# Attention without context in a stage of its own, with all scores of an item at once

## The reference

```
q, k, v = x Wq, x Wk, x Wv              (16 heads of 16; two of the blocks have biases)
s = q k^T / sqrt(16)                    (per head, 128 x 128)
s = s - slope(head) * |row - column|    (second block), or the causal mask (first and third)
p = softmax(s);  a = p v;  y = a Wo + bo + residual
```

## Time and profile before

| what | value |
|---|---|
| median of 3 runs (lowest, highest) | 3216.21 us (3214.78, 3226.16) |
| the profiled execution | 3218.95 us, span 3217.0 us |
| TensorE products busy | 2769.1 us, 86% of the span |
| VectorE, ScalarE, GpSimd busy | 1649.4, 1451.8, 1388.2 us |
| first stage, 1205 to 1400 us: TensorE, VectorE, ScalarE, GpSimd busy; granted clock | 175.55, 101.67, 132.59, 103.69 us; 0.98 |
| second stage, 1735 to 1925 us: the same | 166.08, 135.47, 146.49, 112.75 us; 0.92 |
| third stage, 2720 to 2912 us: the same | 179.34, 106.34, 138.51, 113.24 us; 0.98 |

### The profile page before, as it was taken

The page is one execution under the profiler, slowest core; times in us unless marked ns, Lnnn a source line. Parts: engine busy times, 40 slices in busy tenths (PEclk is TensorE's granted clock), DMA queues, the critical chain, the costliest instruction groups (busy, mean ns, idle before and its releaser), DMA issues. The chain is left out here.

```text
span 3217.0 us, 71298 instructions
## 1 busy us (share of the span) xinstructions
PE 2769.1 (86%) x25153; PEld 2159.4 (67%) x25153; DVE 1649.4 (51%) x3584; ACT 1451.8 (45%) x4618; POOL 1388.2 (43%) x1626
## 2 busy tenths in 40 slices
PE   5888888659989978969984979999994895999999
PEld 5777777546756656655653767877874564777888
DVE  3888889674446655561115762333332222555643
ACT  4565565254446656743325862333231233773310
POOL 2666667352356665543324661233321222663321
PEclk8999999679999999979996988999995997999999
DMA  2000000100000000051111002000006111010100
GB/s 79 2 2 2 2 2 2 42 26 29 19 15 17 16 19 1 0 186 43 45 60 50 0 13 87 10 8 9 10 1 236 46 34 53 1 46 24 54 9 19
DMA packets 70793, 106.17 MB, mean 33 GB/s; under 512 B 10768, under 2 KB 48272, under 8 KB 70304
## 3 DMA queue, kind: packets, MB, share of 16 engines
q1 hardware_dynamic: 64608, 86.68, 7.9%
q0 software_dynamic: 5952, 16.26, 1.6%
HBM read 88.50 MB, written 14.42 MB: 32 GB/s over the span
## 5 line engine op out<-in xcount | busy, mean ns | idle before, releaser
L517 POOL TENSOR_TENSOR probs<-probs,inv 128x512 f32<-128x512 f32 x320 | 328.0, 1039 | 296.5 <-DVE inv L847 296.1
L3316 POOL TENSOR_TENSOR hc<-h,bc 128x1024 f32<-128x1024 f32 x128 | 301.6, 2356 | 185.2 <-DVE h L3580 168.6
L742 ACT ACTIVATE probs<-s_ps,negmax 128x128 f32<-128x128 f32 (+1 forms) x768 | 297.1, 414 | 8.3 <-DVE negmax L807 6.9
L3580 DVE TENSOR_TENSOR_SCAN h<-da,dbu_ps 128x1024 f32<-128x1024 f32 x128 | 292.4, 2284 | 10.3 <-DVE dbu_ps L3592 4.4
L615 PE MATMUL t_ps<-ident,probs 128*128 128x128 f32 x1280 | 208.1, 286 | 56.3 <-POOL probs L517 47.6
L615 PEld LDWEIGHTS t_ps<-ident,probs 128*128 128x128 f32 x1280 | 139.3, 141 | 122.9 <-POOL probs L517 59.1
L3400 PE MATMUL dta_ps<-dt,a_spread 32*128 32x128 f32 x2048 | 163.0, 302 | 45.8 <-ACT da L3527 26.0
L3527 ACT ACTIVATE da<-dta_ps 128x1016 f32<-128x1016 f32 x128 | 130.2, 1017 | 144.3 <-PE dta_ps L3400 143.9
L3592 DVE TENSOR_TENSOR dbu_ps<-dbu_ps,bc 128x1024 f32<-128x1024 f32 x128 | 155.7, 1217 | 71.7 <-PE dbu_ps L3405 71.4
L3400 PEld LDWEIGHTS dta_ps<-dt,a_spread 32*128 32x128 f32 x2048 | 137.1, 203 | 68.8 <-ACT da L3527 31.0
L807 DVE TENSOR_REDUCE negmax<-s_ps 128x4 f32<-128x1024 f32 (+1 forms) x128 | 156.6, 1223 | 46.4 <-PE s_ps L601 44.5
(11 more groups left out here) (509 smaller groups left out, 6871.5 us busy)
## 6 DMA issues: line engine op xcount, KB each, us to landing
c_in<-in_ctx SPq DMA_DIRECT2D x48, 256.0 KB, 2.6
w_up<-in_L_ffn_w SPq DMA_DIRECT2D x8, 1024.0 KB, 12.9
w_down<-in_L_ffn_w SPq DMA_DIRECT2D x8, 1024.0 KB, 11.6
w_gate<-in_L_ffn_w SPq DMA_DIRECT2D x8, 512.0 KB, 9.7
w_up<-in_L_ffn_w SPq DMA_DIRECT2D x8, 512.0 KB, 9.5
w_down<-in_L_ffn_w SPq DMA_DIRECT2D x8, 512.0 KB, 9.8
w_gate<-expert_rows_out SPq DMA_DIRECT2D x8, 512.0 KB, 6.8
wkv<-in_L_xattn_Wkv SPq DMA_DIRECT2D x2, 2048.0 KB, 11.8
```

The lines of the kernel that those rows point to most:

```text
L517: pool.tensor_tensor(probs[:, u % 2, i], probs[:, u % 2, i], inv[:, u % 2, HB * i:HB * (i + 1)].unsqueeze(2).broadcast_to([P, HB, W]), ALU ...
L742: last = act.activation(probs[:, u % 2, i, k, :], src, ACT.Exp, bias=negmax[:, u % 2, at], accum_out=sums[:, u % 2, at])
L3316: pool.tensor_tensor(hc[:, s % 4], h[:, s % 2], bc[:, j, 1, :].unsqueeze(1).broadcast_to([P, 2 * G, P]), ALU.mult).then_inc(hc_ready.sem, 1)
L3580: dve.tensor_tensor_scan(flat(h[:, s % 2]), flat(da[:, s % 4]), dbu_ps[s % 2][:, :, :, :].rearrange("p i g t -> p (i g t)"), 0.0, ALU.mult ...
```

## The change

`local_attention_stage` is a new function for the three blocks without a context; `self_attention_stage` stays for the one over a context. What it does otherwise than before:

- `score(b, j)` makes all 16 heads of an item together, on four strips and into the four banks of `s_ps`; it waits until all exponentials of the item before are done. All four masks come ahead of them.
- On TensorE x is turned and q and k are projected two items ahead, v one item ahead, all at new places in `unit`. `out` follows `project_v` and waits for `v_ready` of the next item.
- VectorE makes all four copies of `t_ps` (before, ScalarE made two), in a new order of its whole queue.
- GpSimd fetches x three items ahead, behind the second `scale` of an item; `save` stands between the last two. The statistics for the fetch (`ahead`) stand behind `take_context(b, j, 0)` on VectorE.
- ScalarE takes q and the turned x ahead of the item's exponentials.

The functions that are not shown below (`turn`, `project_qk`, `project_v`, `row_max`, `exponentiate`, `invert`, `scale`, `fetch`, `residual`, `save`, `finish`, `moments`, `take_k`, `take_v`) do for one item what they did, with `kt` = 1 put in; `project_qk` also waits for `out_used` of item b - 3.

```diff
+def local_attention_stage(core, halves, wq, wk, wv, wo, out_bias, qkv_bias=None, causal=False, alibi=False,
+                         pre_norm=None, target=None, norm=True, after=None):
...
+        def every_item(eng, unit):
+
+            unit(0, 0, True, 2)
+            unit(1, 1, False, 2)
+            with eng.Fori(0, B // 2 - 3) as i:
+                unit(2 * i + 2, 0, False, 2)
+                unit(2 * i + 3, 1, False, 2)
+            unit(B - 4, 0, False, 2)
+            unit(B - 3, 1, False, 2)
+            unit(B - 2, 0, False, 1)
+            unit(B - 1, 1, False, 0)
...
+            def unit(b, j):
+                scale(b, 0, 0)
+                scale(b, 0, 1)
+                if b + 3 < B:
+                    fetch(b + 3, 1 - j)
+                residual(b, j)
+                scale(b, 1, 0)
+                if b >= 2:
+                    save(b - 2, j)
+                scale(b, 1, 1)
+
+            for b in range(2):
+                fetch(b, b)
+            pool.wait_ge(loads.sem, weights)
+            fetch(2, 0)
+            for b in range(B):
+                unit(b, b % 2)
+            save(B - 2, 0)
+            save(B - 1, 1)
...
+            def score(b, j):
+                pe.wait_ge(q_ready.sem, q_ready.done(b))
+                pe.wait_ge(k_ready.sem, k_ready.done(b))
+                pe.wait_ge(exp_done.sem, exp_done.done(2 * NP * b - 1))
+                if alibi:
+                    pe.wait_ge(biased_done.sem, biased_done.done(2 * NP * b - 1))
+                if causal:
+                    for u in range(NP):
+                        for i in range(2):
+                            pe.matmul(s_ps[u][:, i, :], core.ident_bf[:, :], mask[:, :, :].rearrange("p h t -> p (h t)"),
+                                      start=True, stop=False, skip_group_check=True)
+                for k in range(HB):
+                    for u in range(NP):
+                        for i in range(2):
+                            s, qc = pair_heads(1, u, i)[k][0:2]
+                            row = ROWS * (2 * u + i)
+                            last = pe.matmul(s_ps[u][:, i, k * W:(k + 1) * W], q[s][row:row + ROWS, j, qc, :],
+                                             kT[row:row + ROWS, j, qc, :], start=not causal, stop=True,
+                                             skip_group_check=causal)
+                        if k == HB - 1:
+                            last.then_inc(scored.sem, 1)
...
+            def weigh(b, j, u):
+                g = NP * b + u
+                pe.wait_ge(a_ready.sem, a_ready.done(2 * b + u - 1))
+                if u == 0:
+                    pe.wait_ge(v_ready.sem, v_ready.done(b))
+                for i, copied in enumerate((pT_even, pT_odd)):
+                    pe.wait_ge(copied.sem, copied.done(g))
+                    for k, (s, qc, ch, cg, par) in enumerate(pair_heads(1, u, i)):
+                        last = pe.matmul(o_ps[cg * ROWS:(cg + 1) * ROWS, ch, :],
+                                         v[:, j, 4 * ch + cg, par * ROWS:(par + 1) * ROWS], pT[:, u % 2, i, k, :],
+                                         start=(u == 0 and par == 0), stop=(par == 1), skip_group_check=True)
...
+            def out(b, j, ahead):
+                pe.wait_ge(a_ready.sem, a_ready.done(2 * b + 1))
+                pe.wait_ge(v_ready.sem, v_ready.done(ahead))
+                pe.wait_ge(out_used.sem, out_used.done(b - 1))
+                for cc in range(DC):
+                    last = pe.matmul(bank_d[:, 0:DC, :].rearrange("p a t -> p (a t)"), aT[:, j, cc, :],
+                                     wo_sb[:, cc, :], start=(cc == 0), stop=(cc == DC - 1))
+                last.then_inc(out_ready.sem, 1)
+
+            def unit(b, j, first, left):
+                score(b, j)
+                if not first:
+                    turn_probs(b - 1, 1, 1)
+                if left == 2:
+                    turn(b + 2, j)
+                if not first:
+                    weigh(b - 1, 1 - j, 1)
+                if left:
+                    project_v(b + 1, 1 - j)
+                if not first:
+                    out(b - 1, 1 - j, b + 1 if left else b)
+                turn_probs(b, 0, 0)
+                turn_probs(b, 0, 1)
+                if left == 2:
+                    project_qk(b + 2, j)
+                weigh(b, j, 0)
+                turn_probs(b, 1, 0)
+                if not left:
+                    turn_probs(b, 1, 1)
+                    weigh(b, j, 1)
+                    out(b, j, b)
+
+            pe.wait_ge(loads.sem, weights)
+            pe.wait_ge(consts.sem, ready_consts)
+            turn(0, 0)
+            project_qk(0, 0)
+            project_v(0, 0)
+            turn(1, 1)
+            project_qk(1, 1)
+            every_item(pe, unit)
...
+            def unit(b, j, first, left):
+                if left:
+                    take_q(b + 1, 1 - j)
+                if left == 2:
+                    copy_turned(b + 2, j)
+                for u in range(NP):
+                    for i in range(2):
+                        exponentiate(b, u, i)
...
+            def copy_probs(b, u, i):
+                g = NP * b + u
+                dve.wait_ge(p_turned.sem, p_turned.done(2 * g + i))
+                dve.wait_ge(weighed.sem, weighed.freed(g))
+                dve.tensor_copy(pT[:, u % 2, i], t_ps[:, :, :]).then_inc((pT_even, pT_odd)[i].sem, 1)
...
+            def take_context(b, j, ch):
+                dve.wait_ge(weighed.sem, weighed.done(NP * b + NP - 2 + ch))
+                dve.wait_ge(out_ready.sem, out_ready.freed(b))
+                dve.tensor_copy(aT[:, j, ch, :], o_ps[:, ch, :]).then_inc(a_ready.sem, 1)
...
+            def unit(b, j, first, left):
+                row_max(b, 0)
+                if not first:
+                    copy_probs(b - 1, 1, 1)
+                row_max(b, 1)
+                if not first:
+                    take_context(b - 1, 1 - j, 1)
+                invert(b, 0, 0)
+                if left:
+                    take_v(b + 1, 1 - j)
+                invert(b, 0, 1)
+                copy_probs(b, 0, 0)
+                if not first:
+                    finish(b - 1, 1 - j)
+                copy_probs(b, 0, 1)
+                invert(b, 1, 0)
+                if left == 2:
+                    take_k(b + 2, j)
+                take_context(b, j, 0)
+                if left == 2:
+                    ahead(b, j)
+                invert(b, 1, 1)
+                copy_probs(b, 1, 0)
+                if not left:
+                    copy_probs(b, 1, 1)
+                    take_context(b, j, 1)
+                    finish(b, j)
+
+            def ahead(b, j):
+                if pre_norm is not None and (not isinstance(b, int) or b + 3 < B):
+                    pre_moments(b + 3, 1 - j)
+
+            pre_moments(0, 0)
+            pre_moments(1, 1)
+            pre_moments(2, 0)
...
+            take_k(0, 0)
+            take_v(0, 0)
+            take_k(1, 1)
+            every_item(dve, unit)
...
-            first_causal = self_attention_stage(core, a["half_scales"], a["L1_ffn_wq"], a["L1_ffn_wk"], a["L1_ffn_wv"],
+            first_causal = local_attention_stage(core, a["half_scales"], a["L1_ffn_wq"], a["L1_ffn_wk"], a["L1_ffn_wv"],
...
-        with_distances = self_attention_stage(core, a["half_scales"], a["L2_attn_wq"], a["L2_attn_wk"], a["L2_attn_wv"],
+        with_distances = local_attention_stage(core, a["half_scales"], a["L2_attn_wq"], a["L2_attn_wk"], a["L2_attn_wv"],
...
-        causal = self_attention_stage(core, a["half_scales"], a["L3_attn_Wq"], a["L3_attn_Wk"], a["L3_attn_Wv"],
+        causal = local_attention_stage(core, a["half_scales"], a["L3_attn_Wq"], a["L3_attn_Wk"], a["L3_attn_Wv"],
```

308 lines of the change are left out of this document (added).

## The result

The changed kernel takes 3442.07 us (median of 4 runs, 3436.58 to 3448.25), the one before 3221.18 (4 runs). The ratio is 1.0687, its 95% interval 1.065 to 1.0723: 221 us slower, where 166 were forecast. The profiled execution has a span of 3434.8 us, 217.8 above the one before.

The account below looks back on a forecast made before the run. TensorE, which hardly stops within an item, was taken as the bound, with new waits outweighing the saved 1.2 us. Stages +100, +40 and +23 and ends +3 gave +166, 3382 us as a median, range 3340 to 3430 (0.55).

Parts of the forecast that it names:

- Part 1: Scores on four strips: 32 records in 0.99 us, gaining about 1.2 per item in first and third stage, 1.1 in second.
- Part 2: TensorE's new order, third stage: 9.4 us of work and 2.8 of waits, 12.2 per item, where it was 11.24.
- A: Mid-weighing wait of TensorE for VectorE's copy of the bank just turned, behind its row maximum: 1.0 us third stage, 1.9 second.
- Part 3: Second stage, no masks but a longer row maximum: longer waits, period 12.9 us, where it was 11.37.
- B: TensorE's wait ahead of `out` for VectorE's copy of v: 0.8 us in the third stage, 1.4 in the second.
- C: TensorE's wait between the two turns of pair 0, which share `t_ps`: 1.0 us per item.
- Part 4: First stage: GpSimd's fetch and residual ahead of a scale leave TensorE 5.3 us idle per item, in 13 items.
- Part 5: Lower clock behind waits, per item: 2.0 us in the first stage (19.5), 1.3 in the second (14.2), 0.7 in the third (12.9).
- The sum's "before": Old stage times taken as 15 periods, 175.5, 170.6 and 168.6 us, against new 275.9, 211.0 and 191.5: +100, +40, +23.
- The ends: Stage ends: second item's q and k ahead of first scores, 2.0 to 3.7 us per stage; last item about 2 less: +3.
- the third: Rival for the whole kernel: clock low nearly throughout, or strips that overlap only by two: 3430 to 3460 us, chance 0.13.
- Rival 2: Whole kernel with the clock staying high: stages +74, +21 and +12 us, 3326 in all, range 3300 to 3340, chance 0.18.

Follow-up runs that it names:

- experiment 3: Changed kernel with the score loops turned so that two strips are in use at a time, masks still together: 3442.64 us, ratio 1.0696 to the kernel before.
- experiment 2: Changed kernel with unused products put into TensorE's waits in the first and second stage: 3373.47 us, ratio 1.0469 to the kernel before.
- Experiment 6: Changed kernel with both scales of pair 1 ahead of fetch, residual and save on GpSimd: 3368.96 us, ratio 1.0477 to the kernel before.
- experiment 7: Changed kernel with both scales first, `out` between pair 0's turns, last bank's copy on ScalarE, q projected ahead of those turns: 3308.81 us, ratio 1.0268.
- 8: The kernel of experiment 7 with the scores on two strips at a time, by the loops of experiment 3: 3313.28 us, ratio 1.029 to the kernel before.
- experiment 1: Changed kernel with only scale(b, 1, 0) moved ahead of fetch and residual on GpSimd: 3411.44 us, ratio 1.0592 to the kernel before.
- 4: Changed kernel with the output projection of the item before moved between the two turns of pair 0: 3415.61 us, ratio 1.0607 to the kernel before.
- 9: Kernel before the change, with the q projection moved ahead of the turn of bank (1,0), k left behind it: 3251.6 us, ratio 1.01.

## Why the prediction was wrong in its size

The direction was right and so was the mechanism of the waits; the time lies 2 us above the range, 60 above the forecast. The step that failed is the price of the lower clock in the second stage. By the prediction's own parts:

- **Part 1** held in its row and not in its worth. The scores do take about 1.0 to 1.2 for 32 records. That the gain counts in full did not hold: in the third stage two strips give the same period (experiment 3), because a wait follows the scores.
- **Part 2** gave 12.2 for a high clock, 12.13 was measured, and not by luck: from the second half of weighing on, each start lies within 0.2 of the laid-out queue. One wait was placed wrongly: the lateness of `scale(b,1,1)` was said to hide in A, but shows as 0.38 of its own, and A is the shorter for it, since VectorE's row maximum and copy set its end. The 0.7 for the clock was not spent: the third stage's rows are at the higher clock but for its first items, in spite of four waits per item.
- **Part 3**'s waits were right to 0.2 (A 2.05, B 1.57, C 0.87). The period at a high clock is 13.5 (experiments 2 and 3), for 12.9 forecast; the 0.7 by which `out` starts late is most of that.
- **Part 4** was right: 5.27 for 5.3, a period of 19.40 for 19.5, and without the clock 17.55 for 17.5. Experiment 6 takes the chain's 5.27 away, and 5.7 per item with it, the low clock behind it included, against a new 1.46.
- **Part 5, for the second stage, is the step that failed.** It took 1.3 per item for the lower clock and 2.6 as the most. Measured is 3.4 (16.92 less 13.56, experiment 2), in nearly every item. The prediction does not say what work the 2.6 stands for; at its rate of 0.87 it is 3.0 us of it, little more than the second turn, q and k. But the clock is low from `out` on, that is from wait B and not from C. Start to start, beside the same steps of the third stage, `out` takes 1.83 for 0.94, the turn of (0,0) and its copy 1.94 for 1.47, the turn of (0,1) 0.90 for 0.49, q 1.71 for 0.89, k 1.84 for 0.99, which adds to 3.4. The stage took 245.7, where 211.0 was laid out: the clock's 2.1 too little is some 30 us over the full items, the period at a high clock another 9, and its first and last items are shorter.
- **The sum's "before"** was 15 full periods per stage, 11 us more than the stages took.
- **The ends** were put at +3 and came to about +14.5. From q of item 0 to the first scores the stages need 4.7, 1.4 and 4.9 us more than before, 11 together, near the forecast 2.0 to 3.7 per stage. The last item was forecast as 2 shorter in each stage; from its first scores to the last `out` it takes 1.5, 2.3 and 1.2 us more, 5 together. In the third stage TensorE's waits behind these scores add to 6.8 us, where they were 3.4.

In the profiled run 217.8 us were measured for 166. The second stage itself is 35 us above its sum, the first 2 above and the third 9 below, the "before" accounts for 11 and the ends for 11.5.

Of the rivals, the third (clock low nearly throughout or two strips, 3430 to 3460) has the time, but neither half of its mechanism: the strips overlap, and the clock was low for part of each item in two stages, and high in the third. Rival 2 needs the clock high everywhere; experiment 2 nearly made it so and gave 3373, not 3326: from q of item 0 to the last `out` its stages are 92, 39 and 22 us longer than before, its added products included, where the sum at a high clock has 74, 21 and 12, and 3 for the ends.

The figure of the Trainium skill, page "TensorE: Matmul & The Clock Gate", section "Back-to-back issue gap" (about 81 ns for each load and product), is not what these scores take: 37 ns per record on four strips (1.17 for 32) and 54 on two (1.73, from 2992.38 to the end of the last). The same page of the Trainium skill, section "HAM oscillation — how this bites in real kernels", tells of a kernel whose bursts, parted by transfer waits of some 3 to 5 us, start at the lower clock every time. The first stage agrees, with masks of 1.91 behind waits of 5.1 to 5.6. In the second, waits of 2.05 and 1.57 were followed by the lower clock too, and the third's bursts stay high between waits of 0.4 to 0.9.

Why did the saved 1.2 per item not come back in experiment 7, with TensorE's order mended? Its third stage waits on the chain through VectorE and GpSimd, and 8 shows that the strips matter by 0.4 per item in that stage and by nothing in the first. The order of before gives VectorE, ScalarE and GpSimd half an item at a time, and while one half is scored the other is being scaled. All scores at once leave one burst of exponentials and scales per item, to be waited for. That this alone is the 86 us that stay is argued, not shown: no run here has the old order with four strips, and none has VectorE's order mended.

## What to carry to other kernels

Price an order by its copies and handovers, not by its products: 1.2 us of TensorE saved per item came with 2.2 of waits and an item 0.9 longer in the third stage, and with a wait of 5.3 where a fetch got between two scales on GpSimd. Where the trace shows a lower clock behind a wait, price every record up to where it is high again, here from `out` to k and 3.4 us per item, and try unused products in the wait: they took 69 us off this kernel and 3 off the one before. Mend one late producer and look for the next one behind it before counting the gain (experiments 1, 4 and 9).

## What the runs showed of the hardware

The second stage settles in one of two rhythms: 16.9 us per item with `out`, the turns, q and k at the lower clock, in the changed kernel and in experiment 6 in nearly every item, or 13.5 with them at the higher, in most items of experiment 3, which differs there only in the order of the scores. Both occur in one run and with the same code: experiment 3 has 13.5 and 17, and experiment 1 q rows of 1.91 and 1.06 mostly in turn, 15.3 per item on average. Runs of one kernel differ in time and clock together as well: experiment 6 took from 3359.28 us at a mean granted clock of 0.904 to 3400.56 at 0.888. So a small change of order can be worth 50 us in this stage, and a difference of that size between two variants may be the clock's and not the edit's; what tips it from one rhythm to the other no run here shows. The length of one wait does not settle it: in experiment 1 an item with waits of 1.36 and 1.57 kept the higher clock and one with a wait of 2.46 did not, and in the kernel before 1.31 was followed by the lower one.

With the waits filled the granted clock over the whole kernel rose from 0.897 to 0.928. A steady stream of unused f32 products of 128 columns ran at 119 ns a record (14 records from 1955.89 to 1957.55).
